# Whitening 32 images on one core: the final product in four 64x64 tiles, stores from SyncE, ten image buffers

## The chip, the cores and the metric

The kernel runs on one core of one Trainium2 chip. The metric is device time in microseconds (us), the median of several runs. One more execution was taken with the hardware profiler; all rows below come from that one.

## What is computed

The input x is 32 images of 256 channels and 48x48 = 2304 pixels, float32. Channel c belongs to group row c mod 32, so each image is a 32 x 18432 matrix. The reference, cut to what matters:

```python
x1 = x.reshape(N, C // G, G, H, W).transpose(0, 2, 1, 3, 4).reshape(N, G, -1)   # G = 32
xc = x1 - x1.mean(-1, keepdims=True)
cov = xc @ xc.transpose(0, 2, 1) / M + EPS * jnp.eye(G)
decorr = isqrt_newton_schulz(cov, 10)          # Y = Y @ T, Z = T @ Z with T = 0.5 * (3 I - Z @ Y)
y = weight1 @ decorr @ xc + bias1              # back in the order (N, C, H, W)
```

## The kernel before

An image lies in SBUF as 128 partitions x 2 halves x 2304 pixels (`xs`, 18 KB a partition): partition p of half h is channel 128 h + p. There are `SLOTS = 8` such buffers; the result overwrites the image in place. A partition's channel counts mod 32, so one 32x32 matrix, repeated four times on the diagonal of a 128x128 matrix `apply_w`, whitens a half.

The work runs in 19 phases, a pair of images each (`phase(r, c)`, c from 0 to 18). A phase has twelve cells, one for each sixth of each of its two images (a piece, `q` from 0 to 5: 768 columns of one half). Four things go on at once, for different pairs:

- DMA: SyncE loads images. The first 8 go out at the start; image n + 8 is issued when the store of image n has landed (L254 waits, L256 issues), a half at a time.
- ScalarE (ACT), one pair ahead: it sums a part of the image (L274) and adds a shift to it (`centre`, L290, four a image).
- VectorE (DVE): 32x32 transposes of the shifted image (L407, two a piece), and its links of the Newton chain.
- TensorE (PE), a cell: `covariance` of pair c (24 products of 128x32 by 33 columns, L590), one step of the Newton chain of pair c-1 (L563, L567 and others), `output` of pair c-2 (L607: one piece), and the next chain step. The chain has 24 steps (`STEPS`), two a cell: PE makes a small product, DVE reads it (L461, L465), PE needs that for the next.

PE, ACT and DVE each take their work in this written order. A piece of output is two products with a 128x128 `apply_w`, of 512 and 256 columns, into the two banks of one of two PSUM buffers `y_ps` (L607); every float32 product shows as two MATMUL instructions in the trace. ACT adds the bias and writes the piece back to the image (L307). After the third piece of a half ACT waits for its own write and issues the store of the half (L316 to L319); the very last image is stored piece by piece (L312). In phases 16 and 17, where no covariance is left, the two products have 384 columns each (`evenly`).

Phases 0 and 1 fill the pipeline: covariance begins in 0, the chain in 1, output in 2. Phase 16 has the chain of the last pair and the output of pair 14; phase 17 has only the output of pair 15. The chain's first step (GATHER, L544) marks the start of a phase; its last (SPREAD, L573, L575) yields `apply_w` (L418).

Of the kernel before, what the change touches and what calls it, by code (L numbers as in the profile page):

```python
# [39 lines left out]
SLOTS = 8  # L40
# [28 lines left out]
FLAT = PAIR * IMAGE_PIECES  # L69

# [41 lines left out]
def whiten(nc, x, weight, bias, out):  # L112
# [3 lines left out]
    with ctx:  # L116
# [40 lines left out]
        apply_w = sb("apply_w", [P, 2, PAIR, BLOCKS, G])  # L157
# [5 lines left out]
        y_ps = pb("y_ps", [P, 2, 2, BANK])  # L163
# [65 lines left out]
        def evenly(r, c):  # L229

            return isinstance(r, int) and c >= PAIRS

        def by_piece(r, c, i):

            return isinstance(r, int) and (c, i) == (PAIRS - 1, PAIR - 1)

        @block.sync
        def _(sp):
# [27 lines left out]
        def _(act):  # L266
# [25 lines left out]
            def output(r, c, i, q, even):  # L292

                m = IMAGE_PIECES * image(r, c, i) + q
                h, o = q // PIECES, q % PIECES * PIECE
# [4 lines left out]
                slot = xs[slot_of(c, i)]  # L300
                if even:
                    src = y_ps[:, q % 2, :, 0:PIECE // 2]
                    dst = slot[:, h, o:o + PIECE].rearrange("p (t s) -> p t s", t=2)
                else:
                    src = y_ps[:, q % 2].rearrange("p t s -> p (t s)")[:, 0:PIECE]
                    dst = slot[:, h, o:o + PIECE]
                nc.scalar.activation(dst, src, ACT.Identity,  # L307
                                     bias=y_bias[:, c % 2, i:i + 1]).then_inc(y_read, 1)
                if by_piece(r, c, i):

                    act.wait_ge(y_read, m + 1 + 2)
                    act.dma_start(out_v[image(r, c, i), :, h, o:o + PIECE], slot[:, h, o:o + PIECE]).then_inc(  # L312
                        stored[slot_of(c, i)][h], 16)
                elif q % PIECES == PIECES - 1:

                    act.wait_ge(y_read, m + 1 + 2)  # L316
                    n = image(r, c, i)
                    dst = out_v[n, :, h, :] if isinstance(n, int) else out_v[bass.ds(n, 1), :, h, :].rearrange("o p s -> p (o s)")
                    act.dma_start(dst, slot[:, h, :]).then_inc(stored[slot_of(c, i)][h], 16)  # L319
# [11 lines left out]
            def phase(r, c):  # L331
                for f in range(FLAT):
# [4 lines left out]
                    if exists(r, done[0]):  # L337
                        output(r, *done, evenly(r, c))
# [20 lines left out]

            for n in range(SLOTS):  # L360
                for h in range(HALVES):
                    stores = IMAGES // SLOTS + (PIECES - 1 if n == SLOTS - 1 else 0)
                    act.wait_ge(stored[n][h], 16 * stores)

        @block.vector
        def _(dve):
# [48 lines left out]

            def diagonal(dst, src, n, rows, count):

                return nc.vector.tensor_tensor(  # L418
                    dst, src.unsqueeze(2).to_broadcast([rows, n, count, G]),
                    blocks[0:rows, 0:count, :].unsqueeze(1).to_broadcast([rows, n, count, G]), ALU.mult)  # L420
# [101 lines left out]
        def _(pe):  # L522
# [71 lines left out]
            def output(r, c, i, q, part, even):  # L594
# [14 lines left out]
                if part == 1:  # L609
                    ins.then_inc(y_done, 1)  # L610
# [38 lines left out]
```

## Time and profile before

| what | value |
|---|---|
| median of 3 runs | 597.41 us (587.82, 597.41, 600.44) |
| profiled execution, its own time | 590.64 us |
| its span, first to last instruction | 588.8 us |
| mean granted TensorE clock over the span | 0.983 of full speed |
| read from HBM, written to HBM | 75.51 MB, 75.50 MB |

The span is what the rows add up to; 1.8 us of the profiled execution's time lie around it. The engines overlap, so that their busy shares don't add up to the span. What matters is which of them the others wait for, stretch by stretch.

### The profile page before, as it was taken

What the parts mean: (1) busy time and instruction counts of PE and PEld (TensorE: products, weight loads), DVE (VectorE), ACT (ScalarE), POOL (GpSimd) and SP (SyncE); (2) the same over time, 40 slices, a digit from 0 to 9 for tenths busy, and PEclk for the clock granted to TensorE, in tenths of its full rate; (3) what the DMA queues carried; (4) which work ended last, traced back from release to release, by engine and by line L of the source; (5) the groups of instructions that cost most, each with busy time, mean ns of one, the idle gap of its engine ahead of it and who ended that gap; (6) DMA issues with size and microseconds to landing.
All of it is one profiled execution on the core that took longest, in us unless ns stands there. A gap on an engine that the chain in (4) does not pass through costs nothing.

```text
span 588.8 us, 25310 instructions
## 1 busy us (share of the span) xinstructions
PE 510.4 (87%) x11584; PEld 318.8 (54%) x11584; DVE 331.0 (56%) x1037; ACT 348.0 (59%) x450; POOL 0.7 (0%) x6
## 2 busy tenths in 40 slices
PE   3447899899798899979988997998989989998896
PEld 3336655566465566636555654665546655555453
DVE  6747575657366476646655664675647656652210
ACT  5643675667465576746656774675666756533445
POOL 0000000000000000000000000000000000000000
PEclk9999999999899899999999998999989999999999
DMA  8993066868667867966759786788597685443338
GB/s 321 408 422 144 3 244 228 340 242 323 244 243 218 348 254 279 353 248 251 300 193 342 287 318 203 293 291 316 213 333 283 245 302 206 164 164 161 162 160 322
DMA packets 19642, 152.63 MB, mean 259 GB/s; under 512 B 2512, under 2 KB 2512, under 8 KB 3536
## 3 DMA queue, kind: packets, MB, share of 16 engines
q1 hardware_dynamic: 9744, 75.52, 35.7%
q10 hardware_dynamic: 9792, 75.50, 31.8%
q8 instruction: 91, 1.49, 1.0%
q14 instruction: 15, 0.12, 0.1%
HBM read 75.51 MB, written 75.50 MB: 256 GB/s over the span
## 4 chain that ended last, share of the span: by engine, by line
PE 82%; issue 9%; DVE 4%; DMA 2%; ACT 1%; SPq 1%; ACTq 0%; DVEq 0%
PE y_ps L607 48%; PE cov_ps L590 18%; PE chain_ps L567 5%; PE chain_ps L563 5%; DMA b_col<-bias 2%; PE chain_ps L573 2%; PE shift_ps L529 1%; ACT image L307 1%; PE chain_ps L552 1%; DVE transposed L407 1%; DVE outer L439 1%; PE chain_ps L575 1%; PE chain_ps L565 1%; PE chain_ps L559 1%; PE chain_ps L561 1%
## 5 line engine op out<-in xcount | busy, mean ns | idle before, releaser
L607 PE MATMUL y_ps<-image,apply_w 128*128 128x256 f32 (+2 forms) x768 | 304.4, 522 | 1.7 <-ACT image L307 1.1
L307 ACT ACTIVATE image<-y_ps,y_bias 128x768 f32<-128x768 f32 x192 | 172.6, 899 | 182.5 <-PE y_ps L607 168.6
L407 DVE STREAM_TRANSPOSE transposed<-image 128x384 f32<-128x384 f32 x384 | 213.4, 570 | 15.1 <-issue 2.1
L590 PE MATMUL cov_ps<-transposed 128*32 128x33 f32 x9216 | 134.4, 207 | 46.9 <-issue 40.8
L290 ACT ACTIVATE image<-image,shift 128x1152 f32<-128x1152 f32 x128 | 158.5, 1249 | 13.6 <-ACT image L307 10.9
L607 PEld LDWEIGHTS y_ps<-image,apply_w 128*128 128x128 f32 x768 | 133.2, 193 | 35.4 <-ACT image L307 5.2
L590 PEld LDWEIGHTS cov_ps<-transposed 128*32 128x32 f32 x9216 | 110.0, 117 | 57.5 <-issue 50.9
L461 DVE SCALAR_TENSOR_TENSOR t_mat<-chain_ps,eye 64x32 f32<-64x32 f32 x144 | 26.0, 181 | 110.2 <-PE chain_ps L563 108.6
L563 PEld LDWEIGHTS chain_ps<-yz 32*32 32x32 f32 x576 | 20.6, 105 | 109.2 <-issue 95.0
L465 DVE COPY yz<-chain_ps 64x64 f32<-64x64 f32 x144 | 29.6, 206 | 39.1 <-PE chain_ps L567 35.8
L567 PE MATMUL chain_ps<-yz,t_mat 32*32 32x64 f32 x512 | 40.2, 234 | 4.9 <-DVE t_mat L461 3.1
L563 PE MATMUL chain_ps<-yz 32*32 32x32 f32 x576 | 36.9, 206 | 3.1 <-DVE yz L465 2.8
L567 PEld LDWEIGHTS chain_ps<-yz,t_mat 32*32 32x32 f32 x512 | 18.4, 106 | 11.3 <-DVE t_mat L461 4.1
L274 ACT ACTIVATE junk<-image 128x288 bf16<-128x288 f32 x32 | 14.1, 441 | 14.2 <-ACT image L307 10.4
L529 PEld LDWEIGHTS shift_ps<-shift_sum,shift_mat 128*128 128x128 f32 x64 | 12.1, 216 | 14.5 <-issue 11.7
L529 PE MATMUL shift_ps<-shift_sum,shift_mat 128*128 128x1 f32 x64 | 12.2, 260 | 6.8 <-ACT junk L274 6.8
L283 ACT COPY shift<-shift_ps 128x1 f32<-128x1 f32 x32 | 4.9, 153 | 22.2 <-PE shift_ps L529 22.2
L468 DVE TENSOR_SCALAR folded<-chain_ps,col 64x128 f32<-64x128 f32 x16 | 5.5, 343 | 19.5 <-PE chain_ps L561 19.5
L438 DVE COPY d_col<-chain_ps 64x1 f32<-64x1 f32 x16 | 2.4, 150 | 21.7 <-PE chain_ps L545 21.7
L552 PE MATMUL chain_ps<-col,blocks 128*64 128x1 f32 x32 | 4.6, 214 | 8.3 <-DVE cov_sq L444 8.2
L573 PE MATMUL chain_ps<-folded,pick 64*128 64x32 f32 x64 | 10.5, 285 | 1.0 <-DVE folded L468 1.0
L418 DVE TENSOR_TENSOR apply_w<-chain_ps,blocks 128x256 f32<-128x256 f32 x16 | 6.5, 406 | 6.0 <-PE chain_ps L575 6.0
(54 smaller groups left out, 125.0 us busy)
## 6 DMA issues: line engine op xcount, KB each, us to landing
image<-x SPq DMA_DIRECT2D x63, 1152.0 KB, 7.2
y<-image ACTq DMA_DIRECT2D x62, 1152.0 KB, 5.6
y<-image ACTq DMA_DIRECT2D x6, 384.0 KB, 3.4
image<-x SPq DMA_DIRECT2D x2, 576.0 KB, 4.2
w_nat<-weight SPq DMA_DIRECT2D x4, 4.0 KB, 10.2
b_col<-bias SPq DMA_DIRECT2D x4, 0.1 KB, 10.6
```

Source lines behind the costliest of these rows:

```text
L274: nc.scalar.activation(junk[:], xs[slot_of(c, i)][:, 0, 0:SHIFT_PIXELS], ACT.Identity, accum_out=shift_sum[:, i:i + 1]).then_inc(summed, 1)
L290: nc.scalar.activation(part, part, ACT.Identity, bias=shift[:, i:i + 1]).then_inc(centred, 1)
L307: nc.scalar.activation(dst, src, ACT.Identity, bias=y_bias[:, c % 2, i:i + 1]).then_inc(y_read, 1)
L407: nc.vector.transpose(dst, xs[slot_of(c, i)][:, h, of_half:of_half + PIECE // 2]).then_inc(transposed, 1)
L461: link(nc.vector.scalar_tensor_tensor(out=t_mat[:], in0=product, scalar=-0.5, in1=eye15[:], op0=ALU.mult, op1=ALU.add))
L465: link(nc.vector.tensor_copy(yz[:, first:2], following[:, first:2]))
L529: nc.tensor.matmul(shift_ps[:, 0:1], shift_mat[:], shift_sum[:, i:i + 1], start=True, stop=True).then_inc(shift_ready, 1)
L563: ins = nc.tensor.matmul(chain_ps[rows, C_PRODUCT:C_PRODUCT + G], z, y, start=True, stop=True)
L567: ins = nc.tensor.matmul(chain_ps[rows, C_NEXT:C_NEXT + 2 * G], factor, yz[rows].rearrange("p m g -> p (m g)"), start=True, stop=True)
L573: nc.tensor.matmul(chain_ps[:, at:at + G], pick[:, i, :, :].rearrange("p b g -> p (b g)"), folded[:, 0, :], start=True, stop=True)
L590: ins = nc.tensor.matmul(cov_ps[rows, i, 0:G + 1], xt[q][:, t, 0:G], xt[q][:, t, 0:G + 1], start=q == 0 and t < BLOCKS, stop=q == IMAGE_PI ...
L607: ins = nc.tensor.matmul(y_ps[:, q % 2, bank, 0:z - a], apply_w[:, c % 2, i, :, :].rearrange("p b g -> p (b g)"), xs[slot_of(c, i)][:, h, ...
```

## The change

- `SLOTS` goes from 8 to 10.
- The final product: a piece is now a strip of 384 pixels (`STRIP`) of both halves, in place of 768 pixels of one half. It is made by four products of 64 contracted rows and 64 output partitions, one for each pair of a row half and a column half of the array. `apply_w` shrinks to 64x64 blocks (two 32x32 on a diagonal, by a new constant `parity`). Product (row, col) reads image half h = row xor col and writes PSUM partitions of `col` in bank h. So the two row halves write different banks for the same output partitions. For half 1 the result of partitions 0 to 63 comes out in 64 to 127 and the other way round.
- ACT reads both banks in one ACTIVATE (128 x 2 x 384) and writes both halves of the strip. It issues no more DMAs, and doesn't wait for its own write.
- Stores move to SyncE: for each image, after its last piece, half 0 in one DMA of 128 partitions and half 1 in two of 64 partitions, which put the crossed channels back. Loads stand in the same queue: the load of image n + 9 is issued behind the store of image n, when the store of image n - 1 has landed. The last image is stored in three parts, two strips each.
- `evenly`, `by_piece` and `diagonal` go; the final waits for stores move from ACT to SyncE.

```diff
-SLOTS = 8
+SLOTS = 10
+HALF = P // 2
+STRIP = PIXELS // IMAGE_PIECES
-        apply_w = sb("apply_w", [P, 2, PAIR, BLOCKS, G])
+        apply_w = sb("apply_w", [P, 2, PAIR, 2, G])
+        parity = sb("parity", [P, 2, G])
-        y_ps = pb("y_ps", [P, 2, 2, BANK])
+        y_ps = pb("y_ps", [P, 2, HALVES, BANK])
@@ sync
-            for r in range(IMAGES // SLOTS - 1):
-                for n in range(SLOTS):
-                    for h in range(HALVES):
-                        sp.wait_ge(stored[n][h], 16 * r + 16)
-                        src = x_v[SLOTS * r + SLOTS + n, :, h, :]
-                        sp.dma_start(xs[n][:, h, :], src).then_inc(loaded[n][h], 16)
+            def store(n, pieces):
+                sp.wait_ge(y_read, IMAGE_PIECES * n + pieces.stop + 2)
+                cols = slice(STRIP * pieces.start, STRIP * pieces.stop)
+                slot = xs[n % SLOTS]
+                sp.dma_start(out_v[n, :, 0, cols], slot[:, 0, cols]).then_inc(stored[n % SLOTS][0], 16)
+                for rows, channels in ((slice(0, HALF), slice(HALF, P)), (slice(HALF, P), slice(0, HALF))):
+                    sp.dma_start(out_v[n, channels, 1, cols], slot[rows, 1, cols]).then_inc(stored[n % SLOTS][1], 16)
+            def load_next(n):
+                for h in range(HALVES):
+                    sp.wait_ge(stored[n % SLOTS][h], 16 * (1 + h) * (n // SLOTS + 1))
+                    sp.dma_start(xs[n % SLOTS][:, h, :], x_v[n + SLOTS, :, h, :]).then_inc(loaded[n % SLOTS][h], 16)
+            for n in range(IMAGES):
+                if n == IMAGES - 1:
+                    for q in range(0, IMAGE_PIECES, 2):
+                        store(n, slice(q, q + 2))
+                else:
+                    store(n, slice(0, IMAGE_PIECES))
+                if 0 < n <= IMAGES - SLOTS:
+                    load_next(n - 1)
@@ scalar, output
-                nc.scalar.activation(dst, src, ACT.Identity,
-                                     bias=y_bias[:, c % 2, i:i + 1]).then_inc(y_read, 1)
-                if by_piece(r, c, i):
-                    act.wait_ge(y_read, m + 1 + 2)
-                    act.dma_start(out_v[image(r, c, i), :, h, o:o + PIECE], slot[:, h, o:o + PIECE]).then_inc(
-                        stored[slot_of(c, i)][h], 16)
-                elif q % PIECES == PIECES - 1:
-                    act.wait_ge(y_read, m + 1 + 2)
-                    act.dma_start(dst, slot[:, h, :]).then_inc(stored[slot_of(c, i)][h], 16)
+                nc.scalar.activation(xs[slot_of(c, i)][:, :, STRIP * q:STRIP * (q + 1)], y_ps[:, q % 2, :, 0:STRIP],
+                                     ACT.Identity, bias=y_bias[:, c % 2, i:i + 1]).then_inc(y_read, 1)
@@ vector, last step of the chain
-                    link(diagonal(apply_w[:, c % 2], spread, PAIR, P, BLOCKS))
+                    link(nc.vector.tensor_tensor(apply_w[:, c % 2], spread.unsqueeze(2).to_broadcast([P, PAIR, 2, G]),
+                                                 parity[:].unsqueeze(1).to_broadcast([P, PAIR, 2, G]), ALU.mult))
@@ vector, set-up
+            then(nc.vector.tensor_tensor(parity[:], blocks[:, 0:2, :], blocks[:, 2:4, :], ALU.add))
@@ tensor, output
-                bank = 1 - part
-                a, z = BANK * bank, min(BANK * (bank + 1), PIECE)
-                ins = nc.tensor.matmul(y_ps[:, q % 2, bank, 0:z - a], apply_w[:, c % 2, i, :, :].rearrange("p b g -> p (b g)"),
-                                       xs[slot_of(c, i)][:, h, o + a:o + z], start=True, stop=True)
+                for row in range(2):
+                    for col in range(2):
+                        rows, out_rows = slice(HALF * row, HALF * (row + 1)), slice(HALF * col, HALF * (col + 1))
+                        h = row ^ col
+                        ins = nc.tensor.matmul(y_ps[out_rows, q % 2, h, 0:STRIP], apply_w[rows, c % 2, i].rearrange("p k g -> p (k g)"),
+                                               xs[slot_of(c, i)][rows, h, STRIP * q:STRIP * (q + 1)], start=True, stop=True)
+                ins.then_inc(y_done, 1)
```

## Rows read from the trace of the kernel before

**Rows 1.** The page: busy time and share of each engine, then the granted clock.
```profile
PE 510.4 (87%) x11584; PEld 318.8 (54%) x11584; DVE 331.0 (56%) x1037; ACT 348.0 (59%) x450; POOL 0.7 (0%) x6
...
PEclk9999999999899899999999998999989999999999
```
**Rows 2.** The page: each DMA queue's packets, MB, share (q1 loads, q10 stores).
```profile
q1 hardware_dynamic: 9744, 75.52, 35.7%
q10 hardware_dynamic: 9792, 75.50, 31.8%
```
**Rows 3.** L544, first step of the chain, by line: durations, first and last start.
```profile
L544 PE MATMUL chain_ps<-stats,mean_col x64: 197/217/262, 36.1 to 539.7; 128*32 128x33 f32 x64
```
**Rows 4.** Busy us (x instructions) in stretches; last columns: granted clock, DMA share, GB/s.
```profile
64.50:539.70 475.20, 437.64 (x10086) 270.64 (x10088) 282.24 (x856) 289.62 (x375) 0.00 (x0) 0.98 0.70 259
206.58:237.38 30.80, 30.42 (x725) 18.99 (x725) 20.55 (x63) 21.44 (x29) 0.00 (x0) 1.00 0.73 270
341.42:377.75 36.33, 32.00 (x725) 19.71 (x725) 20.67 (x63) 21.44 (x29) 0.00 (x0) 0.95 0.80 289
20.00:32.00 12.00, 5.63 (x312) 5.11 (x304) 10.07 (x24) 5.67 (x9) 0.00 (x0) 1.00 1.01 424
```
**Rows 5.** The chain that ended last, one cell undisturbed, then one disturbed: start, us, what.
```profile
211.38 1.49 PE y_ps L607 x4
212.87 0.18 PE chain_ps L563 x4
213.05 0.56 PE cov_ps L590 x44
213.61 0.23 PE chain_ps L567 x4
213.84 1.49 PE y_ps L607 x4
...
361.09 0.38 PE cov_ps L590 x29
361.46 3.30 issue
364.77 0.54 PE cov_ps L590 x19
365.31 0.35 PE chain_ps L567 x4
365.66 2.65 PE y_ps L607 x4
368.31 0.18 PE chain_ps L563 x4
```
**Rows 6.** Waits over the span: who waited for whom, us in total, times, longest.
```profile
ACT image L290 <- ACT image L307: 10.9, 26, 0.5
ACT junk L274 <- ACT image L307: 10.4, 25, 0.4
SPq L256 <- DMA y<-image: 446.5, 48, 59.7
```
**Rows 7.** The page: DMA issues, count, KB each, median us from issue to landing.
```profile
image<-x SPq DMA_DIRECT2D x63, 1152.0 KB, 7.2
y<-image ACTq DMA_DIRECT2D x62, 1152.0 KB, 5.6
```
**Rows 8.** Timeline, phase 17 on PE: output alone, start, us, count of instructions.
```profile
568.53 11.50 PE L607 MATMUL y_ps<-image,apply_w 128*128 128x384 f32 x35
```
**Rows 9.** Groups of instructions by form: count, busy us, mean ns of one, idle before.
```profile
L407 DVE STREAM_TRANSPOSE transposed<-image 128x384 f32<-128x384 f32 x384 | 213.4, 570 | 15.1 <-issue 2.1 <-PE cov_ps L590 1.5 <-ACT image L290 0.6
L307 ACT ACTIVATE image<-y_ps,y_bias 128x768 f32<-128x768 f32 x192 | 172.6, 899 | 182.5 <-PE y_ps L607 168.6 <-DVE yz L455 13.5 <-ACT image L307 0.4
L590 PE MATMUL cov_ps<-transposed 128*32 128x33 f32 x9216 | 134.4, 207 | 46.9 <-issue 40.8 <-DVE transposed L407 6.0
L567 PE MATMUL chain_ps<-yz,t_mat 32*32 32x64 f32 x512 | 40.2, 234 | 4.9 <-DVE t_mat L461 3.1 <-issue 1.8
L418 DVE TENSOR_TENSOR apply_w<-chain_ps,blocks 128x256 f32<-128x256 f32 x16 | 6.5, 406 | 6.0 <-PE chain_ps L575 6.0
```
**Rows 10.** Timeline, a cell of phase 16: output and two chain steps.
```profile
544.43 0.25 PE L563 MATMUL chain_ps<-yz 32*32 32x32 f32 x4
...
544.80 0.18 DVE L461 SCALAR_TENSOR_TENSOR t_mat<-chain_ps,eye 64x32 f32<-64x32 f32 x1 [1.49 <-PE chain_ps L563]
...
545.04 0.30 PE L567 MATMUL chain_ps<-yz,t_mat 32*32 32x64 f32 x4 [0.35 <-DVE t_mat L461]
...
546.76 0.25 PE L563 MATMUL chain_ps<-yz 32*32 32x32 f32 x4
```
**Rows 11.** Timeline, end of phase 17 on ACT.
```profile
584.64 0.90 ACT L307 ACTIVATE image<-y_ps,y_bias 128x768 f32<-128x768 f32 x1 [0.42 <-PE y_ps L607]
585.57 0.34 ACTq L312 DMA_DIRECT2D y<-image  x1
```
**Rows 12.** Timeline, the first pieces of output: L607 at two speeds.
```profile
66.31 2.93 PE L607 MATMUL y_ps<-image,apply_w 128*128 128x256 f32 x4
...
73.17 1.56 PE L607 MATMUL y_ps<-image,apply_w 128*128 128x256 f32 x4
```
**Rows 13.** Busy us in two stretches behind the standstill of rows 5; columns as in rows 4.
```profile
364.60:367.90 3.30, 3.13 (x27) 1.76 (x27) 0.80 (x2) 0.00 (x0) 0.00 (x0) 0.50 0.41 106
367.98:372.00 4.02, 4.02 (x119) 2.63 (x119) 2.49 (x8) 3.23 (x4) 0.00 (x0) 1.00 0.98 401
```

More of the change, by code:

```diff
@@ L227, in phases @@
                 phase(0, c)
[L229 to L235, printed above, removed]
         @block.sync
@@ L249, in _ @@
                         sp.dma_start(b_col[G * b:G * (b + 1), :], bias[0]).then_inc(consts_in, 16)
-            for r in range(IMAGES // SLOTS - 1):
-                for n in range(SLOTS):
-                    for h in range(HALVES):
-                        sp.wait_ge(stored[n][h], 16 * r + 16)
-                        src = x_v[SLOTS * r + SLOTS + n, :, h, :]
-                        sp.dma_start(xs[n][:, h, :], src).then_inc(loaded[n][h], 16)
+            def store(n, pieces):
[17 more added lines that the diff above has]
+                    load_next(n - 1)
+            for n in range(SLOTS):
+                for h in range(HALVES):
+                    stores = (IMAGES - n + SLOTS - 1) // SLOTS + (IMAGE_PIECES // 2 - 1 if n == (IMAGES - 1) % SLOTS else 0)
+                    sp.wait_ge(stored[n][h], 16 * (1 + h) * stores)
         @block.gpsimd
@@ L290, in centre, with output @@
                 nc.scalar.activation(part, part, ACT.Identity, bias=shift[:, i:i + 1]).then_inc(centred, 1)
-            def output(r, c, i, q, even):
+            def output(r, c, i, q):
                 m = IMAGE_PIECES * image(r, c, i) + q
-                h, o = q // PIECES, q % PIECES * PIECE
                 if i == 0 and q == 0:
@@ L337, in phase @@
                     if exists(r, done[0]):
-                        output(r, *done, evenly(r, c))
+                        output(r, *done)
                     ahead = later(c, i, 2)
@@ L358, in _ @@
             phases(act, phase)
[L360 to L363, printed above, removed]
         @block.vector
@@ L414, in covariance_out @@
                 nc.vector.tensor_copy(stats[:, c % 2, i, :], cov_ps[:, i, 0:G + 1]).then_inc(cov_read, 1)
[L416 to L420, printed above, removed]
             def chain(r, c, t):
@@ L592, in covariance, with output @@
                 ins.then_inc(cov_done, 1)
-            def output(r, c, i, q, part, even):
-                if part == 0:
-                    if i == 0 and q == 0:
-                        pe.wait_ge(chain_dve, DVE_TOTAL * (PERIOD * r + c) + DVE_TOTAL)
-                    pe.wait_ge(y_read, IMAGE_PIECES * image(r, c, i) + q + 1)
-                h, o = q // PIECES, q % PIECES * PIECE
-                bank = 1 - part
-                a, z = BANK * bank, min(BANK * (bank + 1), PIECE)
-                if even:
-                    a, z = PIECE // 2 * bank, PIECE // 2 * (bank + 1)
-                ins = nc.tensor.matmul(y_ps[:, q % 2, bank, 0:z - a], apply_w[:, c % 2, i, :, :].rearrange("p b g -> p (b g)"),
-                                       xs[slot_of(c, i)][:, h, o + a:o + z], start=True, stop=True)
-                if part == 1:
-                    ins.then_inc(y_done, 1)
+            def output(r, c, i, q):
+                if i == 0 and q == 0:
+                    pe.wait_ge(chain_dve, DVE_TOTAL * (PERIOD * r + c) + DVE_TOTAL)
+                pe.wait_ge(y_read, IMAGE_PIECES * image(r, c, i) + q + 1)
+                for row in range(2):
[5 more added lines that the diff above has]
+                ins.then_inc(y_done, 1)
             def phase(r, c):
@@ L620, in phase @@
                     if m == 1 and exists(r, done[0]):
-                        output(r, *done, 0, evenly(r, c))
-                        output(r, *done, 1, evenly(r, c))
+                        output(r, *done)
                     if (c, f, m) == (1, 0, 0):
```

9 lines of the change are left out of this document (removed).

## The prediction, made before the change was run

> **What bounds the kernel now.** I read the page first. TensorE is busy for 87% of the span, VectorE and ScalarE for 56% and 59% [rows 1]; the two DMA queues took 35.7% and 31.8% of the sixteen engines' time, together 67.5% or 397 us [rows 2]. Then the stretches. From the first chain step of phase 2 at 64.5 us to that of phase 16 at 539.7 us there are 14 phases [rows 3] in 475.2 us [rows 4], 33.9 us each. An undisturbed one (206.58 to 237.38) takes 30.8 us with PE busy for 30.4; one at 341.42 takes 36.3 us with the same work [rows 4]. The chain of waits says why. In a good cell PE goes from output (1.49) to a chain step (0.18), covariance (0.56), a chain step (0.23) and the next output without a gap, 2.46 us; in the bad phase it stands still for 3.3 us inside covariance, and the output behind it takes 2.65 us [rows 5]. So PE bounds a phase, and something late costs 3.1 us a phase on top. What is late is probably the image: SyncE waits for a store before each of its 48 steady loads, 446.5 us in all [rows 6], and a load takes 7.2 us and a store 5.6 [rows 7], with only half a phase between the end of a buffer's output and the first need for its next image.
>
> **The output step.** The four MATMULs of a piece at peak take 11.50 us / 35 x 4 = 1.31 us at most [rows 8] (768 columns, 1.28 when nothing is missing); in a cell 1.49, so 0.21 are lost to the changes of shape around it [rows 5]. After the change a piece is 4 x 384 columns over quarter arrays. If four tiles run at once it costs half the streaming, 0.64 us, plus 0.21, plus some 0.02 for starting three more tiles: 0.87 us, 0.62 less. Do they run at once? No row shows 64x64. The nearest show both directions of tiling: 44 to 48 covariance MATMULs, each 207 ns long [rows 9], pass in 0.56 us over four column tiles [rows 5]. Two chain tiles on different row groups have four MATMULs of 234 ns in 0.30 us [rows 9, 10]. The bounds are 0.64 for full overlap and 4 x 0.64 = 2.56 for none; I take full overlap, which the covariance row is nearest to.
>
> The two row halves write the same bank here (different partitions). In the chain rows they do too: rows 0-31 and 32-63 of `chain_ps`, one bank, and 4 x 234 ns still fit in 0.30 us [rows 9, 10]. The Trainium skill, page TensorEngine Tiling (Array Packing), section Gotcha 1: PSUM Pressure, says that different row tiles cannot access one PSUM bank at the same time; by that rule the sum would keep the old output step (a rival below), and this case's chain rows speak against it.
>
> **A phase, engine by engine.** PE: 30.8 - 12 x 0.62 = 23.4 us. ACT: busy 21.4 us [rows 4] with the same ACTIVATE of 899 ns for 768 elements [rows 9]; its idle 0.42 us behind a piece that it stores, 21.3 us over the span [rows 6], goes, but PE bounded the phase, so that gives nothing by itself and only keeps ACT under PE. DVE: 20.6 us [rows 4]; `apply_w` halves, at most 0.2 us a phase [rows 9], nothing. The DMA queues: 397 us / 32 = 12.4 us an image, 24.8 a phase [rows 2]; at the pure load rate of 424 GB/s [rows 4] it would be 2 x 4.72 MB / 424 = 22.3. I take 24.8. The stores of half 1 now move 64 partitions each. That price is in no row: the lower bound is nothing, the upper a doubling, 31.8% of 588.8 us / 64 = 2.9 us an image. The nearest row is the 128-partition store [rows 7], so nothing stands in the sum, and the doubling is a rival. SyncE issues five DMAs an image at some 0.34 us, hidden in its 12 us.
>
> So the DMA queues become the longest, 24.8, with PE, ACT and DVE at 23.4, 21.4 and 20.6. Nothing has slack. The chain will show it: PE to DVE to PE takes 0.61 us when DVE is free [rows 10]; behind a transpose of 0.57 [rows 9] it is 1.18, and its cover on the covariance side is only 0.56 + 0.23 = 0.79 us. That costs between 0 and 0.39 us a cell, 0 to 4.7 us a phase. I lay it on the longest resource: 24.8 to 29.5, middle 27.2 us a phase.
>
> **Buffers and queues.** Ten buffers fill at the start, some 11 us more of loading while outputs don't exist yet: hidden. Later the load of image n + 9 is issued when image n is out, a whole phase before it is needed. In front of it in the one queue stand the store of n and itself, 12.4 us; cover 27. The 3.1 us of lateness go, as long as the queues keep up. Behind the wait for the store of n - 1 stands only the store of n + 1, not due for another half phase.
>
> **The ends.** Up to 64.5 us nothing changes. Phase 16 lasted 568.53 - 539.7 = 28.8 us [rows 3, 8], 12 x 0.62 less is 21.4; its chain steps (0.61) are covered by the output on one side. Phase 17: PE needs 0.64 a piece, ACT 0.90 [rows 11]: 12 x 0.90 = 10.8. Before, 3.2 us followed the last ACTIVATE's end. Now the last two images' stores queue up: 5.9 us each (31.8% of 588.8 / 32), 11.7 from mid phase, less the 5.4 left of it, plus some 1.7 to land: 8 us.
>
> **Sum.** 64.5 + 14 x 27.2 + 21.4 + 10.8 + 8 = 485.5 us of span, 487 with the 1.8 around it. The profiled 590.64 is 1.1% under the median of the runs; I put 490 on the median. Own range of this case: 24.8 to 29.5 us a phase, 454 to 520.
>
> **Rival: half-partition stores at half rate (0.30).** An image's DMA goes from 12.4 to 15.3 us and the queue bounds. First store near 80 us (output begins at 66.3 [rows 12], six cells of 2.3), 22 images with a load each: 80 + 22 x 15.3 = 417; then ten stores of 5.9 + 2.9 = 8.8 us, 505, about 510 with landing and what lies around; up to 530 if the chain's waits come on top. For it: sixteen DMA engines at 1.01 share carry 424 GB/s [rows 4], so there is no spare rate. Against: no row shows a partition range matter. The Trainium skill, page SBUF — State Buffer, section Door 1: The DMA port swizzle, says that partitions 0 to 63 reach 8 of 16 ports and get about half the bandwidth, and that two such DMAs gain 6% together; no run of this kernel shows it yet.
>
> **Rival: row tiles take turns (0.08).** Output stays at 1.28 + 0.21; what is left is the lateness that ten buffers remove. 64.5 + 14 x 31 (the undisturbed phase) + 28.8 (phase 16) + 15.5 (phase 17, 12 x 1.3) + 5 (last stores) + 1.8 = 550 us. For it the shared bank, against it the chain rows.
>
> **Rival, slower: the clock (0.07).** The same output takes 2.93 us instead of 1.56 in its first piece [rows 12], and behind the standstill of 3.3 us [rows 5] the granted clock was 0.50, the level of 1.2 GHz, until about 368 us [rows 13]. PE would now stand still more. A phase wholly at the low level has 12 x (1.9 x 0.87 + 1.9 x 0.56 + 0.6) + 1, some 41 us. It decides from 33.9 = 27.2 + f x 13.8, f = 0.49: PE must spend half its phases low. All low: about 690 us. Against: a cell has 1.84 us of PE work in 2.27, without a long gap. No overlap of tiles at all (2.56 us a piece, near 800) is counted here too.
>
> **How the numbers follow.** The forecast has 0.50, the rivals 0.30, 0.08, 0.07; 0.05 stay for small mixtures of no change. The forecast's range and the half-rate stores make 450 to 535, which leaves the 550, the slower cases and little more outside. A measurement of this kernel tells 2% from no change. Faster: 0.90; within 2%: 0.03; slower: 0.07.
>
> **What would show it.** Right: L607 as 64*64 with a piece in about 0.87 us in the chain; phases of 27 us; DMA share over 0.9; ScalarE over 75% busy; no 3 us standstills. A store of 64 partitions landing as late as one of 128, or loads slowed behind it, shows the first rival. A piece of 1.5 us shows the turns. A granted clock under 0.9 shows the third. I am wrong if phases stay over 30 us with DMA share under 0.8: then the chain between PE and DVE costs more than 4.7 us.

## The result, and the profile after

The changed kernel takes 652.14 us (median of 4 runs, 641.39 to 655.68) against 594.15 us for the kernel before (4 runs): ratio 1.110, 95% interval 1.066 to 1.154. It is slower, and 117 us over the upper end of the widest range, 535 us. The profiled execution has 655.48 us and a span of 653.7 us.

The page of the changed kernel: busy time; the granted clock in 40 slices; the queues; the chain of waits by engine; the two groups of the output and the covariance; the large DMA issues.

```profile
PE 505.8 (77%) x12352; PEld 276.2 (42%) x12352; DVE 329.3 (50%) x1038; ACT 342.4 (52%) x450; POOL 0.7 (0%) x6
...
PEclk9999978756866589578566585859556768885577
...
q1 hardware_dynamic: 20080, 151.02, 68.2%
q8 instruction: 97, 1.59, 0.9%
...
PE 73%; issue 17%; DVE 4%; DMA 2%; ACT 1%; SPq 1%; DVEq 0%
...
L593 PE MATMUL y_ps<-image,apply_w 64*64 64x384 f32 x1536 | 244.6, 710 | 7.9 <-issue 7.0
L578 PE MATMUL cov_ps<-transposed 128*32 128x33 f32 x9216 | 161.1, 228 | 90.0 <-issue 85.0
...
image<-x SPq DMA_DIRECT2D x63, 1152.0 KB, 11.9
y<-image SPq DMA_DIRECT2D x31, 1152.0 KB, 4.7
y<-image SPq DMA_DIRECT2D x62, 576.0 KB, 7.3
```

Against [rows 1] no engine is fuller than before: PE 77% for 87%, ScalarE 52% for 59%. DMA is as full as before (68.2% for 67.5% in [rows 2]). What is new: "issue", time in which PE waits for nothing that the profile shows, is 17% of the chain (9% before), 85 us of it ahead of covariance products (40.8 in [rows 9]), and the granted clock is low in most slices.

Stretches of the changed kernel, columns as in [rows 4]: the 14 phases, two stretches inside them at the low level, one at the high level, and one in phase 16.

```profile
68.50:596.00 527.50, 434.57 (x10758) 236.04 (x10759) 280.38 (x856) 284.68 (x375) 0.00 (x0) 0.70 0.67 222
200.50:227.80 27.30, 23.26 (x478) 12.48 (x478) 12.43 (x38) 12.97 (x18) 0.00 (x0) 0.50 0.70 222
309.70:337.00 27.30, 25.70 (x531) 14.11 (x534) 12.70 (x41) 13.51 (x19) 0.00 (x0) 0.50 0.71 235
299.60:309.60 10.00, 7.10 (x235) 3.80 (x222) 7.56 (x22) 7.41 (x10) 0.00 (x0) 1.00 0.90 311
586.20:630.00 43.80, 37.49 (x323) 14.39 (x327) 8.65 (x43) 14.71 (x19) 0.00 (x0) 0.50 0.39 123
```

A phase takes 527.5 / 14 = 37.7 us (33.9 before). Its clock is 0.70, that is (1 - 0.70) x 2 = 60% of the time at 1.2 GHz. One low stretch of 27.3 us has PE busy for 25.7.

The chain of waits of the changed kernel around one pause: start us, us, what.

```profile
301.71 0.81 PE y_ps L593 x8
302.52 0.18 PE chain_ps L551 x4
302.70 0.26 PE cov_ps L578 x14
302.96 1.34 issue
304.29 0.50 PE cov_ps L578 x34
304.80 0.23 PE chain_ps L555 x4
305.03 0.81 PE y_ps L593 x8
305.83 0.18 PE chain_ps L551 x4
306.01 0.56 PE cov_ps L578 x45
306.57 0.23 PE chain_ps L555 x4
306.80 0.81 PE y_ps L593 x8
307.61 0.18 PE chain_ps L551 x4
307.79 0.25 PE cov_ps L578 x13
308.04 2.68 issue
310.72 0.76 PE cov_ps L578 x35
311.48 0.35 PE chain_ps L555 x4
311.83 1.49 PE y_ps L593 x8
```

The edit itself did what was forecast: a piece of output takes 0.81 us where it took 1.49, and a cell 1.78 where it took 2.46. But PE stands still for 1.34 us and, some 5 us later, for 2.68 us, in the middle of a covariance; during the second the clock falls and the piece takes 1.49 us again.

**What the pauses are.** A covariance waits for data at its first product only, so a stop behind the 14th or 13th of its 48 MATMULs (each product is two) is no wait for an image. Read from the trace, the stops of before and after lie 128 MATMULs apart or a multiple of that, give or take a few; 128 MATMULs with their weight loads are 256 instructions. Queue q8, kind "instruction", moves packets of 16384 bytes, 97 of them (91 before), which is 12352 / 128 (11584 / 128), rounded up. One such packet starts between 307.7 and 308.5 us, as the stop of 2.68 us begins:

```profile
q8 instruction: 1, 0.02, 7.6%
```

It lands at 309.31 us, and PE goes on at 310.72. All 31 stops of over 1 us with "issue" as their cause after the change end 1.2 to 1.6 us after a packet of this queue has landed; so do all 12 of before. TensorE's program comes in blocks over the same sixteen DMA engines as the images, and a stop is a block that came late. An undisturbed cell of 60 MATMULs in 2.46 us uses a block in 5.2 us; after the change 64 in 1.78 us use one in 3.6. With the stops and the low clock in it, the blocks land 6.1 us apart in the mean before and 6.3 after: that is the pace at which they were used, not what the queue could do.

### The profile page after: what moved, and what is told of

It reads as the page before. It is cut to its first block, busy times and chain, and to the rows that moved or that the text cites. A ratio compares the mean times of both kernels' runs of the same rounds, so it can differ in the third digit from the quotient of the medians.

```text
span 653.7 us, 26883 instructions
## 1 busy us (share of the span) xinstructions
PE 505.8 (77%) x12352; PEld 276.2 (42%) x12352; DVE 329.3 (50%) x1038; ACT 342.4 (52%) x450; POOL 0.7 (0%) x6
## 3 DMA queue, kind: packets, MB, share of 16 engines
q1 hardware_dynamic: 20080, 151.02, 68.2%
## 4 chain that ended last, share of the span: by engine, by line
PE 73%; issue 17%; DVE 4%; DMA 2%; ACT 1%; SPq 1%; DVEq 0%
PE y_ps L593 35%; PE cov_ps L578 20%; PE chain_ps L555 6%; PE chain_ps L551 5%; PE chain_ps L561 2%; PE shift_ps L517 2%; DMA b_col<-bias 2%; DVE transposed L399 1%; ACT image L315 1%; PE chain_ps L540 1%; PE chain_ps L563 1%; PE chain_ps L547 1%; PE chain_ps L553 1%; PE chain_ps L549 1%; PE chain_ps L532 1%
## 5 line engine op out<-in xcount | busy, mean ns | idle before, releaser
L593 PE MATMUL y_ps<-image,apply_w 64*64 64x384 f32 x1536 | 244.6, 710 | 7.9 <-issue 7.0
L578 PE MATMUL cov_ps<-transposed 128*32 128x33 f32 x9216 | 161.1, 228 | 90.0 <-issue 85.0
L578 PEld LDWEIGHTS cov_ps<-transposed 128*32 128x32 f32 x9216 | 132.6, 138 | 107.0 <-issue 97.5
L593 PEld LDWEIGHTS y_ps<-image,apply_w 64*64 64x64 f32 x1536 | 51.3, 170 | 38.5 <-issue 21.6
L555 PE MATMUL chain_ps<-yz,t_mat 32*32 32x64 f32 x512 | 48.5, 274 | 9.9 <-issue 6.7
L551 PE MATMUL chain_ps<-yz 32*32 32x32 f32 x576 | 42.0, 227 | 9.3 <-issue 6.4
L555 PEld LDWEIGHTS chain_ps<-yz,t_mat 32*32 32x32 f32 x512 | 21.6, 122 | 18.1 <-issue 7.3
L517 PE MATMUL shift_ps<-shift_sum,shift_mat 128*128 128x1 f32 x64 | 16.7, 330 | 6.8 <-ACT junk L290 6.8
L561 PE MATMUL chain_ps<-folded,pick 64*128 64x32 f32 x64 | 14.5, 359 | 1.0 <-DVE folded L454 1.0
L561 PEld LDWEIGHTS chain_ps<-folded,pick 64*128 64x128 f32 x64 | 12.5, 273 | 2.0 <-DVE folded L454 1.2
```

The lines of the kernel that those rows point to most:

```text
L517: nc.tensor.matmul(shift_ps[:, 0:1], shift_mat[:], shift_sum[:, i:i + 1], start=True, stop=True).then_inc(shift_ready, 1)
L551: ins = nc.tensor.matmul(chain_ps[rows, C_PRODUCT:C_PRODUCT + G], z, y, start=True, stop=True)
L555: ins = nc.tensor.matmul(chain_ps[rows, C_NEXT:C_NEXT + 2 * G], factor, yz[rows].rearrange("p m g -> p (m g)"), start=True, stop=True)
L561: nc.tensor.matmul(chain_ps[:, at:at + G], pick[:, i, :, :].rearrange("p b g -> p (b g)"), folded[:, 0, :], start=True, stop=True)
L578: ins = nc.tensor.matmul(cov_ps[rows, i, 0:G + 1], xt[q][:, t, 0:G], xt[q][:, t, 0:G + 1], start=q == 0 and t < BLOCKS, stop=q == IMAGE_PI ...
L593: ins = nc.tensor.matmul(y_ps[out_rows, q % 2, h, 0:STRIP], apply_w[rows, c % 2, i].rearrange("p k g -> p (k g)"), xs[slot_of(c, i)][rows, ...
```

## A balance of the 14 phases

Three numbers per kernel do most of the explaining: the fastest phase as its work (30.3 us with the old output, the fastest phase of before; 22.5 with the tiles, the fastest phase of e2 below), all TensorE gaps of over 0.1 us from 66 us to the end of the span (5 to 14 us of them lie outside the 14 phases), read from the trace, and the time at the low level, (1 - clock) x 2 x stretch, of which 0.4 is lost (a tile cell takes 1.78 us at the high level and 2.9 at the low one, 1 - 1.78 / 2.9). The last two columns are the sum and what the trace has.

| kernel | 14 x work | gaps (those over 1 us) | 0.4 x low | sum | measured |
|---|---|---|---|---|---|
| before | 424 | 42 (24) | 8 | 474 | 475.2 |
| after | 315 | 99 (80) | 127 | 541 | 527.5 |
| e1 whole-array output | 424 | 49 (29) | 8 | 481 | 480.6 |
| e2 a twelfth of the stores | 315 | 52 (35) | 57 | 424 | 421.1 |
| e4 transfers in thirds | 315 | 76 (51) | 75 | 466 | 466.1 |
| e5 old queues, 8 buffers | 315 | 117 (94) | 118 | 550 | 528.9 |
| e14 whole-partition stores | 315 | 85 (66) | 93 | 493 | 486.2 |
| e15 before, half stores | 424 | 51 (29) | 16 | 491 | 492.4 |
| e16 all stores half | 315 | 101 (83) | 117 | 533 | 523.4 |

So the tiles did save 109 us of work in these phases. Gaps (+57) and low clock (+119) took 176 back; the sum is 13 us too high for the changed kernel, since gaps and low stretches overlap: 33 us of its gaps lie in low stretches, and 0.4 of them are counted twice. In e5 part of the gaps is no late block; see there.

## The experiments

"Pauses" are TensorE gaps of over 1 us. All but 1 to 3 us of them have "issue" as their cause, save in e5, e12 and e15. Ratios are to the kernel before, run beside each. Of two runs the profile is of the longer in e2, e4, e5, e6, e7, e12 and e16. The code is abridged.

**e1: the tiles undone, the rest of the change kept.**

```
-apply_w = sb("apply_w", [P, 2, PAIR, 2, G])      +[P, 2, PAIR, BLOCKS, G], with blocks for parity
-4 products 64x64 (row, col)                      +for h in range(HALVES): one product 128x128, 384 columns
-half 1 stored as 2 x 64 partitions               +one store of 128 partitions
```

> The changed kernel with the tiles alone undone: each strip in two products of 128x128 by 384 columns, one for each half, stores of 128 partitions; ten buffers and SyncE's single queue stay (TILE is 34 in place of 36, to make room). Tile theory (four 64x64 products don't bring TensorE's clock back after a pause, full-array ones do): granted clock back to 0.95 or more, time 575 to 600 us, near the kernel before. Pause theory (the faster cell alone makes TensorE outrun its own instruction supply): pauses of over 1 us back to some 20 in number, time 575 to 600 as well, but then the light-traffic run must be fast. Queue theory (one queue for loads and stores, or the half-partition stores, cost the time): with the single queue left 620 us or more if it is the queue; 590 if it was the half-partition stores.

To make room, a row of the transposed tiles shrinks from 36 to 34 numbers. 604.84 us, ratio 1.036 (1.030 to 1.043), clock 0.983. The rest of the change (one queue, ten buffers, strips of both halves) brings no gain and costs 3.6%; the pauses (29 us) stay. The stretch of the 14 phases of e1:

```profile
67.50:548.10 480.60, 436.87 (x10086) 270.31 (x10087) 282.14 (x856) 287.30 (x375) 0.00 (x0) 0.98 0.63 243
```

The balance puts some 7 us of that on gaps and 3 us on the start (67.5 for 64.5); the rest was not followed up. The low clock came with the tiles and their stores.

**e5: the tiles kept, queues and buffers as before.**

```
-SLOTS = 10                      +SLOTS = 8
-sp: store(n, ...); load_next    +sp: loads only; act: the image's stores behind its last piece
```

> The tiles alone: the changed kernel with eight buffers, loads alone in SyncE's queue, stores issued by ScalarE after the last piece of an image (the two half-partition stores among them). Tile theory and pause theory: clock 0.70 to 0.80 and 630 to 670 us, as with the whole change. Queue theory: under 600 us.

653.84 us, ratio 1.118 (1.111 to 1.125), pauses 94 us: the changed kernel's time within its error, as the tile and pause theories had it. But it is not the same loss. The chain by engine of e5, and who PE waited for:

```profile
PE 64%; issue 13%; ACTq 11%; ACT 6%; DVE 3%; DMA 2%; SPq 1%; DVEq 0%
...
PE shift_ps L506 <- ACT junk L267: 40.6, 23, 5.2
```

Read from the trace, only 49 of the 94 us are late blocks (79 after the change) and 41 are waits for ScalarE: for its pass over an image, as in the last row, which counts short waits too, or for its reading of a piece. ScalarE issues the stores here, the half ones in 1.04 us each in the median, and comes late with its own work. So e5 shows that the tiles are slow without the single queue too. Whether that queue adds to the late blocks, e5 can't tell, since it brings a loss of its own.

**e2 and e4: lighter and shorter transfers.** e2 stores 192 of a row's 2304 columns and leaves the rest of the output unwritten; e4 moves the same bytes, each image half loaded and stored in three column parts, each part stored as soon as its two strips are out.

```
e2 -cols = slice(STRIP * pieces.start, STRIP * pieces.stop)   +slice(STRIP * pieces.start, STRIP * pieces.start + STRIP // 2)
e4 -one dma_start a half                                      +for part in three thirds: dma_start(... part ...)
```

> The changed kernel, but each store DMA writes only its first 192 columns of each row part (a twelfth of the image; the rest of the output is left out). Pause theory: TensorE's pauses inside a covariance go away since its instructions no longer wait behind data, the clock stays near 1.0, phases take 22 to 25 us and the time is 430 to 480 us. Tile theory: few pauses, but the clock still lies at 0.5 for long stretches, mean under 0.85, time 520 us or more. Queue theory: time falls below 500 and the granted clock may stay low.

> The changed kernel with every steady load and every store cut into three column parts (rows of 3 KB in place of 9 KB), stores as soon as two strips are out. If an instruction fetch waits for the data transfer ahead of it on its DMA engine as a whole, shorter ones let it through sooner: pauses over 1 us in the steady part from 28 to 15 or fewer, time 600 to 630. If it waits in proportion to the bytes queued whatever their cut, no change: 645 to 665.

e2: 533.45 us (527 to 540), e4: 579.53 (571 to 588). The same products, 97 blocks of instructions each; pauses 35 and 51 us. The stretches of e2, then of e4:

```profile
68.50:489.60 421.10, 375.93 (x10758) 212.72 (x10759) 277.96 (x856) 280.95 (x375) 0.00 (x0) 0.83 0.39 139
```

```profile
68.80:534.90 466.10, 396.50 (x10756) 219.94 (x10757) 279.32 (x856) 283.42 (x375) 0.00 (x0) 0.80 0.76 254
```

Less traffic shortens the pauses, and the clock rises with that. It does not end them: the 430 to 480 us of the pause theory were missed, and time and clock of e2 are where the tile theory had them. e4 shortens the pauses with no byte less. That a block waits less where the transfers ahead of it are short is the likely reason; that the stores start earlier and lie more evenly is another, and no run here parts the two. The pauses are fewer only by 31 to 23 in the phases (15 or fewer expected), yet the time is 20 us under the expected 600. That brings the tiles back to about the time of the kernel before (584 to 589 us in these comparisons), no further.

**e3 and e6: more work in the output step**, to ask whether the quarter arrays as such lower the clock. e3 adds one whole-array product of 384 columns a piece, e6 issues the four tile products twice.

```
e3 +nc.tensor.matmul(y_ps[:, q % 2, 0, 0:STRIP], eye[:], eye[:].unsqueeze(1).to_broadcast([P, 3, P]), ...)
e6 -for row in range(2):      +for again, row in ((0, 0), (0, 1), (1, 0), (1, 1)):
```

> The changed kernel plus one 128x128 product of 384 columns a piece (identity by identity, overwritten at once by the real result), so that TensorE streams as long in full-array form as it did in the kernel before for one half. Tile theory: the clock comes back within some 3 us after each pause, mean 0.93 or more, and in spite of 0.64 us more work a cell the time falls to 560 to 600 us. Pause theory: the output step is 1.45 us as before, so TensorE uses its instructions up more slowly, few pauses, time 580 to 600 with clock near 0.95. Queue theory: time stays at 640 or rises. If low levels still last 7 to 30 us, the tile theory is wrong.

> The changed kernel with the four 64x64 products of each piece issued twice (the second time over the same result), so TensorE streams as long as with a full-array filler, but only in tiles. Tile theory: denser work in tiles doesn't bring the clock back, low stretches of 7 to 30 us stay, mean clock under 0.85 and time 720 us or more. Density theory (any denser stream does it): low stretches of 3.4 us as with the full-array filler, mean clock 0.95 and time about 660 us.

e3: 671.40 us, ratio 1.148 (1.142 to 1.155), clock 0.953, pauses 47 us; the tile and the pause theory had the time at 600 us or less, but the added product costs 0.84 us in each of 192 cells, 161 us. e6: 693.65 us (685 to 702), clock 0.895, pauses 82 us. Read from the trace, a stretch at the low level lasts 4.6 us in the mean in e3, 5.5 in e6, 17.1 after the change and 4.1 before. e6 has only tiles in its output and as many pauses as the changed kernel, yet leaves the low level three times as soon (its theories had 3.4 us, or 7 and more). So the shape of the products alone doesn't hold the clock down. Both runs have about twice the output streaming in a cell; what the chip measures stays open.

**e7 and e9: fewer instructions.** The covariance in 12 products of 64 weights by 65 columns (its two diagonal 32-blocks are used, as two parities) in place of 24 of 32 by 33; on the changed kernel (e7) and on the one before (e9).

```
-for t in range(TILES):                +for t in range(TILES // 2):
-    rows = slice(G * (t % BLOCKS), G * (t % BLOCKS + 1))
+    rows = slice(2 * G * (t % 2), 2 * G * (t % 2 + 1))
-    matmul(cov_ps[rows, i, 0:G + 1], xt[q][:, t, 0:G], xt[q][:, t, 0:G + 1], ...)
+    matmul(cov_ps[rows, i, 0:2 * G + 1], xt[q][:, t, 0:2 * G], xt[q][:, t, 0:2 * G + 1], ...)
```

> The changed kernel with the covariance of a piece in 12 products of 128x64 by 65 columns in place of 24 of 128x32 by 33: TensorE issues 40 MATMULs a cell in place of 64, for the same result. Pause theory: the instruction supply (16 KB fetches, one for 128 MATMULs, at 6 to 9 us each when the DMA engines are full) no longer runs short, pauses of over 1 us in the steady part from 28 to under 8, and the time falls below 600 us even where the clock is low for longer than before; with the clock back to 0.95 it would be 470 to 500. Tile theory: if the pauses go, the clock falls less often, but where it falls it stays low 7 us or more. Queue theory: no change from 650.

> The kernel before with the same wide covariance (36 MATMULs a cell in place of 60), nothing else changed. Pause theory: the pauses inside covariance were late instructions and not late images, so the 22.7 us of pauses over 1 us go and the phase comes near its undisturbed length plus some 0.1 us a cell for the wider products: 31.5 us, time 555 to 570. If the pauses were late images (my prediction's reading), they stay and the time is 590 to 600.

e7: 505.57 us, ratio 0.860 (0.852 to 0.867), pauses 10 us. e9: 591.47 us (10 runs), ratio 1.002 (0.996 to 1.007), pauses 1.0 us. The page of e9, its instruction queue and its chain, and then a cell of its chain:

```profile
q8 instruction: 56, 0.92, 0.6%
...
PE 90%; DVE 3%; DMA 2%; ACT 1%; issue 1%; SPq 1%; ACTq 0%; DVEq 0%
```

```profile
305.72 0.85 PE cov_ps L596 x24
306.57 0.23 PE chain_ps L573 x4
306.80 1.49 PE y_ps L613 x4
308.29 0.18 PE chain_ps L569 x4
```

This is the main run on what the 3.1 us a phase were. Loads, stores and eight buffers are those of the kernel before; the instructions are fewer, 56 blocks for 91. "Issue" falls from 9% of the chain to 1%. The time stays, as the wider covariance takes 0.85 us for 0.56, where 0.1 more was expected: 12 x 0.29 = 3.5 us a phase, what the pauses had cost. So by its time alone e9 looks like the late images (590 to 600 us expected), but those would have kept the pauses. A rival is left in e9 by itself: a cell that is 0.29 us longer also gives a late image 3.5 us more a phase. Against it stand the place of the stops, in the middle of a covariance, their ends behind the landings of q8, and e1, where ten buffers give the images more cover and the stops stay. In e7 the same edit meets a cell that was short of blocks, and gains 147 us. The stretch of its phases, 389.3 / 14 = 27.8 us each:

```profile
58.20:447.50 389.30, 373.49 (x6862) 236.94 (x6863) 279.61 (x856) 284.77 (x375) 0.00 (x0) 0.98 0.87 301
```

**e13: more instructions in the kernel before.** Twelve products of 32 x 32 by one column a piece.

```
+for k in range(12):
+    rows = slice(G * (k % BLOCKS), G * (k % BLOCKS + 1))
+    nc.tensor.matmul(y_ps[rows, q % 2, 1, BANK - 1:BANK], eye[:, rows], eye[:, 0:1], start=True, stop=True)
```

> The kernel before with twelve more tiny products a piece (32x32 by 1 column, into an unused PSUM column, overwritten next time): 24 MATMULs more a cell, 84 in place of 60, and some 0.2 to 0.3 us more of TensorE time, nothing else. By TensorE's time alone: phases of 33.9 + 3 us, 625 to 640 us with pauses as before. By the pause theory TensorE uses up its 16 KB fetches 1.3 times as fast: pauses over 1 us rise from 24 us to 60 us or more, time 650 to 700 us.

658.98 us, ratio 1.128 (1.116 to 1.140). The expected pauses did not come: 16 us. The rise is that of the tiny products themselves, 0.30 us a cell in its chain:

```profile
302.55 0.30 PE y_ps L604 x24
302.84 1.49 PE y_ps L610 x4
```

The products also lengthen the cell. Undisturbed it has 84 MATMULs in 2.76 us and uses a block in 4.2 us, where before it was 5.2; in the mean of a phase (38.0 us) it is 4.8 for 6.0. So TensorE takes its blocks a fifth faster than before, and the stops for late blocks still fall, from 22.7 to 13.7 us. The pace at which instructions are used does not make pauses by itself; the changed kernel wants a block in 3.6 us, and has other stores.

**e14, e15, e16: the stores of 64 partitions.** e14 takes them out of the changed kernel, e15 puts them into the kernel before, e16 makes all stores of the changed kernel such. In e14 the two channel halves of an image's second half come out exchanged.

```
e14 -for rows, channels in (...): dma_start(out_v[n, channels, 1, cols], slot[rows, 1, cols])
    +dma_start(out_v[n, :, 1, cols], slot[:, 1, cols])
e15 -dma_start(out_v[n, :, h, :], slot[:, h, :])      +h = 1: for rows in two halves: dma_start(out_v[n, rows, h, :], slot[rows, h, :])
e16 -dma_start(out_v[n, :, 0, cols], slot[:, 0, cols])  +for rows in two halves: dma_start(out_v[n, rows, 0, cols], slot[rows, 0, cols])
```

> The changed kernel with the second half of an image stored by one 128-partition transfer in place of two 64-partition ones. The channels of that half then come out exchanged in the output (64 to 127 ahead of 0 to 63); the tiles, the ten buffers and the SyncE queue stay, and TensorE's instructions are the same 12352 products. Theory A (the half-partition stores hold the DMA engines longer, so the 16 KB instruction fetches come late, TensorE stands still, and its clock falls behind each pause): pauses of over 1 us fall from 80 us to between 20 and 40 us, the stretches at the low clock from 360 us to under 200 us, and the time from 652 us to 540 to 590 us. Rival B (the stores' form is not what matters; 128 short products are over in 3.7 us and the fetch is late whatever the stores do): pauses stay at 65 to 95 us and the time within 3% of 652 us. Rival C (the tiles' low clock needs no pauses): pauses fall as in A but the low-clock stretches stay over 300 us, and the time stays above 610 us.

> The kernel before with one thing added: the second half of each image (but the last, which goes by pieces) is stored by two transfers of 64 partitions in place of one of 128. Same output, same products. Theory A: pauses of over 1 us rise from 24 us to 45 to 90 us and the time from 594 us to 610 to 650 us; as TensorE runs full-array output products the low-clock stretches stay short (under 6 us each in the mean). Rival B: pauses stay at 15 to 35 us, the phase at 34 us, and the time within 2% of the kernel before.

> The changed kernel with the first half of an image stored by two 64-partition transfers too: twice as many half-partition stores as in the changed kernel. Theory A: pauses of over 1 us rise from 80 us to over 100 us and the time from 652 us to 680 us or more; DMA-engine time rises from 446 us by 40 to 65 us. Rival B: pauses stay at 65 to 95 us and the time within 3% of 652 us.

e14: 614.78 us, ratio 1.056 (1.040 to 1.073). e15: 616.34 us, ratio 1.060 (1.022 to 1.097). e16: 645.06 us (638 and 652; the profile is of the longer). The stretch of the phases of e14, of e15, of e16:

```profile
69.20:555.40 486.20, 407.69 (x10759) 224.53 (x10760) 279.36 (x856) 283.55 (x375) 0.00 (x0) 0.76 0.62 241
```

```profile
64.50:556.90 492.40, 448.38 (x10084) 275.88 (x10084) 281.18 (x856) 288.79 (x375) 0.00 (x0) 0.96 0.76 250
```

```profile
68.00:591.40 523.40, 429.08 (x10756) 234.29 (x10756) 280.18 (x856) 284.63 (x375) 0.00 (x0) 0.72 0.73 224
```

None came out as theory A had it. Taking the half stores out gives 37 of the 58 us back, but pauses only fall from 80 to 66 us (20 to 40 expected), and doubling them adds nothing (pauses 83, time -1%: rival B). In the kernel before they cost 21 us of the span, 17 in the phases and 4 behind them (610.0 - 556.9 for 588.8 - 539.7), but the stops for late blocks are 21.7 us there, as before (22.7). What grew is in the chain by engine of e15:

```profile
PE 73%; issue 9%; ACT 6%; ACTq 6%; DVE 4%; DMA 2%; SPq 1%; DVEq 0%
```

ScalarE and its queue are 12% of it, for 1% and 0% before: it issues two half stores in a typical 0.47 and 0.61 us (at most 2.8) where it issued a whole one in 0.34, and comes late with what PE waits for. So e15 mostly prices the issue of half stores on a busy ScalarE. In the changed kernel, where SyncE issues them, the half stores are one part of the loss, less than half of the excess pauses. And e14 against e1, whose stores and queues are the same, shows the tiles alone, but for the 34 in place of 36: 109 us of work saved, 36 us more gaps and 85 more lost to clock, and the phases end up 5.6 us longer.

**e10, e11, e12: variants of e7.** e10 adds e4's transfers in thirds, e11 stores half 1 by one transfer of 128 partitions as e14, e12 goes back to eight buffers.

```
e10 = e7 + e4      e11 = e7 + e14      e12 = e7 with -SLOTS = 10 +SLOTS = 8
```

> The wide-covariance kernel (tiles, ten buffers, one queue) with every steady load and store in three column parts, stores as soon as two strips are out. The wide-covariance kernel had its DMA engines at a share of 0.99 in the steady part and 505 us. If the DMA engines are its bound in bytes, earlier and shorter transfers only fill the gaps: 495 to 505 us. If shorter rows cost, 510 to 520. If its remaining bound is TensorE, 500 to 507 and no change of the phase of 27.8 us.

> The wide-covariance kernel with half 1 stored by one DMA of 128 partitions in place of two of 64, which leaves its two channel halves swapped in the output. If half-partition stores run at a lower rate (first rival of the prediction), the two queues' engine time falls from 427 us by 30 to 90 us and, since the DMA engines bound this kernel, phases fall from 27.8 to 25 to 26.5 us and the time to 470 to 490 us. If they cost nothing: 500 to 507 us.

> The wide-covariance kernel with eight image buffers in place of ten, all else kept. Loads are then issued a pair later against their need: in SyncE's order the load of image n + 7 stands behind the store of image n, which leaves about no lead. If ten buffers matter once TensorE is fast, ScalarE waits for loads and the time rises to 540 to 620 us; if eight suffice, 505 to 515 us.

e10: 483.69 us (476.64 to 485.76), ratio 0.821 (0.810 to 0.833), pauses 1.0 us. It is the best version, 18% faster than the kernel before, and 11 us under what was expected. e11, whose output is exchanged as that of e14: 487.86 us, ratio 0.835 (0.828 to 0.842), within the 470 to 490 expected; its pauses are 1.0 us too, with whole transfers. The expectation gives e7 a DMA share of 0.99; over the phases it is 0.87, as in the stretch of e7 above. The stretch of most phases of e10, and a cell:

```profile
68.00:440.00 372.00, 365.68 (x6810) 230.66 (x6802) 277.42 (x855) 285.12 (x375) 0.00 (x0) 0.99 0.93 322
```

```profile
302.49 0.81 PE y_ps L602 x8
303.30 0.18 PE chain_ps L560 x4
303.48 0.85 PE cov_ps L587 x24
304.33 0.23 PE chain_ps L564 x4
```

Its clock is 0.99 over the phases: with no pauses the tiles do not lose it, quarter arrays or not, here with the wider covariance. e12: 854.29 us, ratio 1.462, a phase of 52.8 us, far beyond the 540 to 620 us expected. The waits of e12 over the span:

```profile
ACT junk L291 <- DMA image<-x: 339.7, 27, 14.4
```

This is what late images look like: ScalarE waits for them 27 times by name. With one queue, a load stands behind the store of the image after, and eight buffers leave no cover for that; ten do.

## Why the prediction was wrong, step by step

- **"What is late is probably the image": the step that failed.** The 3.30 us of "issue" in [rows 5] sit behind the 29th of the 48 MATMULs of one covariance, where nothing waits for an image, and no wait for a load is among [rows 6]: what SyncE waits for there are stores. They were late instructions (the place of the stops, the landings of q8, e9). I took a queue's long wait for the cause of PE's stop, though the row said "issue" and not "DMA image". So the ten buffers had nothing to remove (e1: no gain), "no 3 us standstills" was wrong, and, worse, the stops grew under the faster cell (28 us of late blocks in e1, 64 in e14, same transfers).
- **The output step, right.** 0.87 us forecast, 0.81 measured (the 0.02 for three more tiles had no row); PE's work of a phase 23.4 forecast, 22.5 at the fastest in e2. The four tiles run at once.
- **Row tiles take turns: refuted.** Each bank is written by both row halves and a piece is 0.81 us, where two tiles at a time would need at least 1.28. The Trainium skill's rule (TensorEngine Tiling (Array Packing), Gotcha 1: PSUM Pressure) that different row tiles cannot access a bank at the same time did not hold in this use.
- **Half-partition stores, right in direction, not the bound.** The rival's sign came true: a store of 64 partitions and 576 KB lands after 7.3 us, one of 128 and 1152 KB after 4.7. In engine time the halves cost 84.6% x 505.2 - 79.0% x 485.0 = 44 us (e7 against e11), and 63 in the changed kernel (68.2% x 653.7 - 62.8% x 609.1), where the rival had up to 32 x 2.9 = 93; on the time 18 us and 37. The Trainium skill, page SBUF — State Buffer, section Door 1: The DMA port swizzle, has 64 partitions at about half the bandwidth of 128. This case agrees in direction; the extra is half to two thirds of what that factor would make. The queues did not bound the changed kernel: DMA share 0.67 in the phases. That sign (phases over 30 us, share under 0.8) was named, but with another cause, the chain between PE and DVE.
- **The clock, the rival that came true.** Its arithmetic held: it decides at f = 0.49 of the phases at the low level, the trace has 0.60. Its chance, 0.07, rested on "2.27 us without a long gap", which is the failed step again. Before, that low stretch lasts 3.4 us behind the pause [rows 13]; I did not ask whether the shorter output would leave it as soon. It took 17 us in the mean.
- **Phases and ends.** 27.2 us a phase forecast, 37.7 measured: what the sum had at nothing, pauses behind the change and a low clock, comes to 7 and 9 us a phase in the balance (99 / 14 and 127 / 14). e10, without pauses, has 26.5 with a covariance that is 3.5 us longer. The chain between PE and DVE cost less than allowed for. The end from phase 16 on: 21.4 + 10.8 + 8 = 40 us forecast, 653.7 - 596.0 = 57.7 measured, of which 44 at the low level by the trace.

What stays open: why in e13 and e15 the stops for late blocks do not grow, when both add to the demand or the load that should lengthen them; how much of the changed kernel's pauses is the faster cell and how much the traffic, the single queue included; and what makes the low level last with the tiles.

## What to carry to other kernels

Before giving a stop of PE to a late transfer, look at where it sits: between two products of one group, with "issue" as its cause, it can't be data; count the instructions between the stops and compare with the instruction queue. A cell that gets shorter with the same number of instructions wants them faster: make products wider when making them quicker (e7: the same tiles went from +11% to -14%). And price a faster step with the stops that it will uncover, and with the clock behind them.

## What the runs showed of the hardware

- TensorE's instructions come in blocks of 16 KB, one for 128 MATMULs with their loads, over the engines that move the data; when one came late PE stood still, 31 times in the changed kernel, for 1 to 5 us, until 1.2 to 1.6 us after it landed. Transfers in thirds, with earlier stores, took pauses from 80 to 51 us (e4), and from 10 to 1.0 with the wide covariance (e10).
- A store of 64 partitions took longer to issue than one of 128: a typical 0.47 us for the first of two and 0.61 for the second, at most 2.8, for 0.34 (e15, on ScalarE's queue).
- Behind a pause the clock went to 1.2 GHz for 3.4 us in the kernel before (once 6.8), and for up to 34 us inside the phases of the changed one, with PE busy for 25.70 of 27.30 us in one of them.
- Four 64x64 tiles on two row and two column halves, 384 columns each, take 0.81 us together, where the two whole-array products they replace take 1.49. A covariance product of 64 weights by 65 columns costs 1.5 times the two of 32 by 33 that it replaces: 0.85 us for 24 MATMULs, 0.56 for 48.
